# A two-layer decoder on one core: the causal mask added on two blocks instead of three, and one sum of each rotary job moved from VectorE to GpSimd

## The chip, the core and the metric

The kernel runs on one core of one Trainium2 chip. The metric is the device time of one execution in microseconds (us), the median of several. Engines are named as in the profile: PE is TensorE, PEld its weight loads, DVE is VectorE, ACT is ScalarE, POOL is GpSimd, SP is SyncE.

## What is computed

Two decoder layers on x (4 batches x 256 positions x 256). Each layer adds attention, a selective state space branch (fed by a context tensor and gated by x) and a feed-forward part. The change lies in attention 1, the attention of the second layer:

```python
qkv = einsum('bsh,oh->bso', x, w_qkv)          # 16 query heads, 4 key/value heads, 128 wide
q, k = layernorm(q, qn_g, qn_b), layernorm(k, kn_g, kn_b)      # per head
q = q * cos + rotate_half(q) * sin             # the same for k
scores = einsum('bhqd,bhkd->bhqk', q, k) / sqrt(D)
scores = where(causal, -inf, scores)           # 256 x 256, triu with k=1
attn = einsum('bhqk,bhkd->bhqd', softmax(scores), v)
x = x + einsum('bsd,od->bso', attn, w_o)
```

Beside it the kernel runs the state space branch of the same layer, a scan over 256 positions for each of 16 states of each batch:

```python
state = state * exp(d_t * A) + (d_t * u_t) * B_t;  y_t = sum_n(state * C_t)
```

## The kernel before, in words

The program is written by engine: each engine has one queue of instructions, carried out in order, with semaphores between engines. In attention 1 all five queues follow one list, `ATT1_PLAN`, that `att1_plan` (L1867) works out when the program is built. Every engine walks the list and issues its own part of each entry, so the list is the order on each queue.

**Units.** One unit is one head of one batch, 64 in all (`u` from 0 to 63). The scores of a unit are a [128, 384] piece of one PSUM bank: columns 0 to 127 are the first 128 queries against the first 128 keys, columns 128 to 383 the second 128 queries against all 256 keys. So two of the three 128 x 128 blocks lie on the diagonal. `s1` (L1711) first writes the mask there with a matmul of a bf16 identity and `mask1` (triangle, zeros, triangle; L1718, `start=True`), then adds the two fp32 products (L1719, L1720, `start=False`). `max1` (L1283) takes the two row maxima on DVE, `exp1` (L777) the exponentials on ACT, `norm1` (L1291) the reciprocal and two scalings on DVE (L1294, L1296, L1297), `pt1` transposes on PE, `pt_copy` copies on ACT (L791), `pv1` multiplies by V on PE, `at_copy` copies on ACT (L797), `o1` adds the output projection on PE (L1750).

**Slots.** The planner spreads these parts over slots. Slot u holds, in this order: the scores of unit u+1; the transposes of a rotary job and their copies, if one is due; norm of unit u-1; pv and copy of unit u-2; max and exp of unit u; o of unit u-3; a projection, if due; the accumulations of the state space steps of the slot before; ACT's decays; the transpose of unit u-1; then the rope, rot and sum parts that are due; last, the state space steps of this slot. So DVE starts each slot with norm of u-1 (which waits for exp of u-1) and max of u, and the start of L1294 number u-1 (from 0) is the start of DVE's slot u.

**Rotary jobs.** There are 20, five for each batch (one for the four key heads, four for the query heads, four heads each), in two tiles `job_a`, `job_b` of [128, 2, 512] fp32. `project` puts a job in PSUM (PE, L1671), ACT squares it (L757). Then DVE does `job` (two products with the tables, L1257, and L1261 twice), `job_sum` (sums of squares, L1269), and later `job_rope`: it adds `job_b` to `job_a` (L1274), waits for that sum and for the reciprocal standard deviations, and does eight multiply-adds (L1280). The standard deviations come from POOL, `job(j)` at L455: a scaling (L459) and a power (L460), started by the sums. PE transposes the job (L1708). A job projected in slot s has rot and sum in s+1, rope in s+3, transposes in s+5 (jobs 0 and 1, which run ahead of the first unit, have the rope in the slot right after the sum, and the second, at s-7, one slot later than the first). Jobs are due every third slot, for units of a batch that starts at slot 0: projections in 0, 3, 6, 9, a V projection in 12, and again one in 13.

**State space steps.** Steps 10 to 63 of the 64 quarter steps lie in attention 1. One step on DVE is a product (L997, into PSUM) and a scan (L1006). POOL then multiplies by C (`times_cq`, L403), and PE accumulates it (L1435). A `times_cq(q)` stands on POOL's queue where step q+1 stands in the list. SP loads the B and C rows, eight steps ahead.

**The planner's costs.** The planner gives DVE's parts a price in us (`rot` 2.6, `sum` 1.2, `rope` 3.2, `step` 2.0) and PE's load of each slot another. It hands out steps so that DVE's total, up to each slot, follows PE's (L1908 to L1947):

```python
spent += sum(price(p) for p in mine)
while ssm and spent + price(ssm[0]) / 2 < total * sum(load[:u + 1]) / sum(load):
    spent += price(ssm[0])
    now.append(ssm.pop(0))
```

For the kernel before, in the slots 0 to 15 of a batch: one step each in 0, 2, 3, 5, 6, 8, 9, 11, 12 and 15 and three in 13 (the same in the slots 16 to 47; from 48 one each in 48, 50, 51, 53, 55, 56, 57, two in 58, one each in 59, 60, 61 and three behind, two of them in 62 and one in 63).

Of the kernel before, what the change touches and what calls it, by code (L numbers as in the profile page):

```python
# [10 lines left out]
ALU = mybir.AluOpType  # L11
# [4 lines left out]
P = 128  # L16
# [73 lines left out]
def build(nc, io, out):  # L90
    ctx = ExitStack()
    with ctx:
        def sb(name, shape, dt=F32):
            return ctx.enter_context(nc.sbuf_tensor(name, shape, dt))

        def sem(name):
            return ctx.enter_context(nc.semaphore(name))
# [50 lines left out]
        identb = sb("identb", [P, P], BF16)  # L148
        mask0 = sb("mask0", [P, W0 + P], BF16)
        mask1 = sb("mask1", [P, 3 * P], BF16)  # L150
# [80 lines left out]
        job_a = lambda j: JA[j % 2]  # L231
        job_b = lambda j: V1[1] if j == 1 else JB
# [23 lines left out]
        ps = ctx.enter_context(nc.psum_tensor("ps", [P, 8, 512], F32))  # L256
# [22 lines left out]
        s = {n: sem(n) for n in names}  # L279
# [97 lines left out]
        def _(pool):  # L377
            gp = nc.gpsimd
# [76 lines left out]
            def job(j):  # L455

                pool.wait_ge(s["job_sum"], j + 1)
                st = jst[:, j % 2]
                ch.link(gp.tensor_scalar(st[:, 1, :], st[:, 0, :], 1.0 / D1, 1e-5, ALU.mult, ALU.add))  # L459
                gp.tensor_tensor(st[:, 2, :], st[:, 1, :], mhalf[:], ALU.pow).then_inc(s["job_rstd"], 1)  # L460

            for kind, a in ATT1_PLAN:
                if kind == "sum":
# [19 lines left out]
            z = slice(512, 1024)  # L483
# [405 lines left out]
        def _(dve):  # L889
            v = nc.vector  # L890
# [320 lines left out]
            step = iter(range(Q_IN_FFN))  # L1211
# [58 lines left out]

            def job_rope(b, i):
                j, x = JOB[b, i], 0 if i else 1
                dve.wait_ge(s["job_rot"], 3 * (j + 1))
                v.tensor_tensor(job_a(j), job_a(j), job_b(j), ALU.add).then_inc(s["job_add"], 1)  # L1274
                dve.wait_ge(s["job_add"], j + 1)
                dve.wait_ge(s["job_rstd"], j + 1)
                for t in range(2):
                    for h in range(REP1):
                        c = slice(D1 * h, D1 * h + D1)
                        v.scalar_tensor_tensor(job_a(j)[:, t, c], job_a(j)[:, t, c], jst[:, j % 2, 2, REP1 * t + h:REP1 * t + h + 1],  # L1280
                                               tabs[:, 3 * x + 2, t, :], ALU.mult, ALU.add).then_inc(s["job_rope"], 1)
# [48 lines left out]
            z = slice(0, 512)  # L1330
# [50 lines left out]
            with dve.Fori(0, E // WRING, 1) as i:  # L1381
                for k in range(WRING):
                    p = k % 2
# [12 lines left out]
        def _(pe):  # L1396
            mm, tr = nc.tensor.matmul, nc.tensor.transpose
# [170 lines left out]
            step = iter(range(6, LAYER_STEPS))  # L1568
# [53 lines left out]
            step = iter(range(Q_IN_FFN))  # L1622
# [88 lines left out]
            def s1(u):  # L1711
                b, h = u // H1, u % H1
                g, p = h // REP1, u % 2
                pe.wait_ge(s["job_tr_copied"], 2 * max(JOB[b, 0], JOB[b, 1 + g]) + 2)
                if u >= 2:
                    pe.wait_ge(s["s1_exp"], 2 * (u - 1))
                q, k = QT[(4 * b + g) % 2], KT[b % 2]
                mm(ps[:, 2 + p, 0:3 * P], identb[:], mask1[:], start=True, stop=True, skip_group_check=True)  # L1718
                mm(ps[:, 2 + p, 0:P], q[:, h % REP1, 0:P], k[:, g, 0:P], start=False, stop=True, skip_group_check=True)  # L1719
                mm(ps[:, 2 + p, P:3 * P], q[:, h % REP1, P:S], k[:, g, :], start=False, stop=True, skip_group_check=True).then_inc(s["s1_mm"], 1)  # L1720

# [145 lines left out]
def att1_plan():  # L1867
# [31 lines left out]
    for b in range(B):  # L1899
# [4 lines left out]
        if b + 1 < B:  # L1904
            rope_job(u + 6, b + 1, 0)
            rope_job(u + 9, b + 1, 1, 3, 4)
            v_job(u + 12, b + 1)
    cost = {"rot": 2.6, "sum": 1.2, "rope": 3.2, "step": 2.0}  # L1908
    ssm = [("da", (m, d)) for m in range(Q_IN_FFN, Q_IN_FFN + 3) for d in range(DT)]
    for m in range(Q_IN_FFN, QSTEPS):  # L1910
        if m + 3 < QSTEPS:
# [150 lines left out]
```

## Time and profile before

| what | us |
|---|---|
| median of 3 executions | 912.32 (912.07 to 913.70) |
| the profiled execution, its own time | 913.75 |
| its span, first to last instruction | 912.0 |
| DVE busy over the span | 703.3 (77%) |
| PE busy over the span | 767.7 (84%) |
| ACT busy | 445.6 (49%) |
| POOL busy | 340.6 (37%) |
| attention 1 (first L1671 to the last residual, L1319) | 334.9 to 674.3 |

Busy is the time with an instruction under way. A timeline row gives start, duration, engine, line, what it writes and reads, how many instructions are merged in it, and in brackets the idle time of that engine ahead of it with what ended it. Durations of neighbouring DVE instructions overlap a little, since the next begins while the last one drains; from start to start is the honest length.

### The profile page before, as it was taken

What the parts mean: (1) busy time and instruction counts of PE and PEld (TensorE: products, weight loads), DVE (VectorE), ACT (ScalarE), POOL (GpSimd) and SP (SyncE); (2) the same over time, 40 slices, a digit from 0 to 9 for tenths busy, and PEclk for the clock granted to TensorE, in tenths of its full rate; (3) what the DMA queues carried; (4) which work ended last, traced back from release to release, by engine and by line L of the source; (5) the groups of instructions that cost most, each with busy time, mean ns of one, the idle gap of its engine ahead of it and who ended that gap; (6) DMA issues with size and microseconds to landing.
All of it is one profiled execution on the core that took longest, in us unless ns stands there. A gap on an engine that the chain in (4) does not pass through costs nothing.

```text
span 912.0 us, 12288 instructions
## 1 busy us (share of the span) xinstructions
PE 767.7 (84%) x3984; PEld 563.1 (62%) x3984; DVE 703.3 (77%) x1229; ACT 445.6 (49%) x928; POOL 340.6 (37%) x242
## 2 busy tenths in 40 slices
PE   6771459877798996799999999999955799999997
PEld 2241346554433563477767776777743689999996
DVE  4869779889857976999999999999977544444443
ACT  1663368650336402666566556756642354444442
POOL 1001346552330422233333323432343286666663
PEclk9785579998799998999999999999987899999999
DMA  4313223345020212011111211111300243334431
GB/s 171 121 47 114 93 94 125 115 139 218 1 98 0 74 43 92 19 40 44 51 36 36 69 36 36 55 39 36 118 0 1 79 158 138 138 138 138 141 135 46
DMA packets 28884, 74.63 MB, mean 82 GB/s; under 512 B 3633, under 2 KB 6337, under 8 KB 28449
## 3 DMA queue, kind: packets, MB, share of 16 engines
q1 hardware_dynamic: 28384, 71.51, 23.2%
q10 hardware_dynamic: 448, 2.49, 0.8%
q8 instruction: 25, 0.41, 0.2%
q14 instruction: 27, 0.21, 0.1%
HBM read 72.55 MB, written 1.44 MB: 81 GB/s over the span
## 4 chain that ended last, share of the span: by engine, by line
PE 50%; DVE 26%; issue 11%; ACT 9%; POOL 3%; DMA 1%; POOLq 0%; DVEq 0%; SPq 0%; ACTq 0%
PE ps L1671 6%; PE ps L1785 6%; PE ps L1786 6%; PE ps L1787 6%; PE ps L1631 4%; DVE hS L976 3%; PE ps L1651 3%; PE ps L1750 3%; PE ps L1435 2%; PE ps L1738 2%; DVE arena L1280 2%; DVE hS L1006 2%; DVE ps L968 2%; PE ps L1408 1%; PE ps L1720 1%
## 5 line engine op out<-in xcount | busy, mean ns | idle before, releaser
L403 POOL TENSOR_TENSOR hS<-hS,BCb 128x512 f32<-128x512 f32 x64 | 81.6, 1278 | 131.9 <-issue 66.7
L1387 DVE SCALAR_TENSOR_TENSOR arena<-ps,arena 128x1024 f32<-128x1024 f32 x32 | 39.2, 1224 | 102.2 <-ACT arena L842 93.1
L426 POOL TENSOR_TENSOR hS<-hS,BCb 128x1024 f32<-128x1024 f32 x23 | 56.1, 2440 | 111.3 <-DVE ps L968 96.3
L1671 PE MATMUL ps<-WB,hT 128*128 128x512 f32 x192 | 88.0, 603 | 3.0 <-DVE arena L1261 2.0
L476 POOL TENSOR_TENSOR MHl<-arena,MHh 128x1024 fp32r<-128x1024 f32 x34 | 81.7, 2404 | 16.9 <-ACT MHh L845 16.9
L1416 PE MATMUL ps<-ident,hS 128*128 128x128 f32 x256 | 40.1, 311 | 54.7 <-POOL hS L426 31.2
L1785 PE MATMUL ps<-Wh,MHh 128*128 128x256 f32 x272 | 77.8, 286 | 6.0 <-POOL MHl L476 6.0
L1006 DVE TENSOR_TENSOR_SCAN hS<-dA,ps 128x512 f32<-128x512 f32 x64 | 78.1, 1220 | 2.2
L1786 PE MATMUL ps<-Wl,MHh 128*128 128x256 f32 x272 | 77.6, 285 | 0.0
L1787 PE MATMUL ps<-Wh,MHl 128*128 128x256 f32 x272 | 77.5, 285 | 0.0
L1416 PEld LDWEIGHTS ps<-ident,hS 128*128 128x128 f32 x256 | 32.6, 159 | 65.1 <-POOL hS L426 38.2
L473 POOL TENSOR_TENSOR Wl<-WB,Wh 128x512 fp32r<-128x512 f32 x34 | 47.3, 1392 | 64.2 <-ACT Wh L826 64.2
L1750 PE MATMUL ps<-WA,arena 128*128 128x256 f32 x256 | 65.7, 380 | 0.0
L1671 PEld LDWEIGHTS ps<-WB,hT 128*128 128x128 f32 x192 | 36.9, 194 | 40.6 <-issue 38.4
L976 DVE TENSOR_TENSOR_SCAN hS<-dA,ps 128x1024 f32<-128x1024 f32 x23 | 52.6, 2286 | 8.2 <-ACT dA L591 7.5
L1785 PEld LDWEIGHTS ps<-Wh,MHh 128*128 128x128 f32 x272 | 52.7, 194 | 8.3 <-POOL MHl L476 7.1
L605 ACT ACTIVATE dA<-DEL,negA 128x255 f32<-128x255 f32 x128 | 55.4, 504 | 0.0
L1785 PE MATMUL ps<-hTh,Wh 128*128 128x512 f32 x136 | 53.8, 396 | 0.0
L1786 PE MATMUL ps<-hTl,Wh 128*128 128x512 f32 x136 | 53.5, 394 | 0.0
L1786 PEld LDWEIGHTS ps<-Wl,MHh 128*128 128x128 f32 x272 | 52.8, 194 | 1.2
L1787 PE MATMUL ps<-hTh,Wl 128*128 128x512 f32 x136 | 53.1, 390 | 0.0
L1787 PEld LDWEIGHTS ps<-Wh,MHl 128*128 128x128 f32 x272 | 52.7, 194 | 0.0
(233 smaller groups left out, 1967.4 us busy)
## 6 DMA issues: line engine op xcount, KB each, us to landing
BCb<-bc_dram SPq DMA_DIRECT2D x32, 512.0 KB, 3.7
BCb<-bcq_dram SPq DMA_DIRECT2D x64, 256.0 KB, 3.1
arena<-gate_dram SPq DMA_DIRECT2D x32, 512.0 KB, 3.7
WB<-in_we SPq DMA_DIRECT2D x34, 256.0 KB, 2.7
WB<-in_wqkv SPq DMA_DIRECT2D x1, 3072.0 KB, 12.7
WA<-in_wo ACTq DMA_DIRECT2D x1, 2048.0 KB, 7.7
WA<-in_ffn SPq DMA_DIRECT2D x1, 1408.0 KB, 7.9
pkb<-in_pk SPq DMA_DIRECT2D x2, 698.0 KB, 4.7
```

The source lines that it names most:

```text
L403: gp.tensor_tensor(h, h, qbc(q)[:, 1:2, :].broadcast_to([P, DT, S]), ALU.mult).then_inc(s["c_ready"], 1)
L426: gp.tensor_tensor(h, h, BCb[g % SB_LOADS][:, 1:2, :].broadcast_to([P, DT, HALF]), ALU.mult).then_inc(s["c_ready"], 1)
L476: gp.tensor_tensor(MHl[:, p, :], MH[p], MHh[:, p, :].bitcast(F32), ALU.subtract).then_inc(s["m_lo"], 1)
L605: sc.activation(qring(dA, q)[:, d, 1:S], DEL[:, d, S * b + 1:S * b + S], ACT.Exp, scale=negA[:, d * DS + n:d * DS + n + 1]).then_inc(s["da ...
L976: v.tensor_tensor_scan(f(h), f(a), f(dbu(g)), 0.0, ALU.mult, ALU.add).then_inc(s["scan_done"], 1)
L1006: v.tensor_tensor_scan(f(qring(hS, q)), f(qring(dA, q)), ps[:, DBQ_BANK, :], 0.0, ALU.mult, ALU.add).then_inc(s["scan_done"], 1)
L1416: last = mm(ps[:, ACC_BANK + j // 2, 256 * (j % 2) + P * d:256 * (j % 2) + P * d + P], src[:, d, P * j:P * j + P], ident[:], start=(first ...
L1671: last = mm(ps[:, bank + t, :], hT[:, c, P * (2 * b + t):P * (2 * b + t) + P], WB[:, c, c0:c0 + 512], start=(c == 0), stop=(c == HC - 1))
L1750: last = mm(ps[:, 5, 256 * t:256 * t + 256], aT1[u % 2][:, P * t:P * t + P], WO1[:, h, :], start=(h == 0 and t == 0), stop=(h == H1 - 1), ...
L1785: mm(out, wh, xh, start=start, stop=False, **kw)
L1786: mm(out, wh, xl, start=False, stop=False, **kw)
L1787: return mm(out, wl, xh, start=False, stop=stop, **kw)
```

## The change

Three edits. The mask matmul writes and reads only blocks 0 and 2 of the three, through a strided view; its `start=True` stays. The sum `job_a + job_b` goes from DVE's `job_rope` to POOL's `job(j)`, behind the power, with the wait for the three products ahead of it; DVE keeps the wait for `job_add`. And the planner's price of `rope` goes from 3.2 to 2.1.

```diff
@@ POOL, job(j)
                 ch.link(gp.tensor_scalar(st[:, 1, :], st[:, 0, :], 1.0 / D1, 1e-5, ALU.mult, ALU.add))
                 gp.tensor_tensor(st[:, 2, :], st[:, 1, :], mhalf[:], ALU.pow).then_inc(s["job_rstd"], 1)
+                pool.wait_ge(s["job_rot"], 3 * (j + 1))
+                gp.tensor_tensor(job_a(j), job_a(j), job_b(j), ALU.add).then_inc(s["job_add"], 1)
@@ DVE, job_rope(b, i)
                 j, x = JOB[b, i], 0 if i else 1
-                dve.wait_ge(s["job_rot"], 3 * (j + 1))
-                v.tensor_tensor(job_a(j), job_a(j), job_b(j), ALU.add).then_inc(s["job_add"], 1)
                 dve.wait_ge(s["job_add"], j + 1)
                 dve.wait_ge(s["job_rstd"], j + 1)
@@ PE, s1(u)
-                mm(ps[:, 2 + p, 0:3 * P], identb[:], mask1[:], start=True, stop=True, skip_group_check=True)
+                diagonal = lambda z: z.rearrange("p (k n) -> p k n", k=3)[:, 0::2, :]
+                mm(diagonal(ps[:, 2 + p, 0:3 * P]), identb[:], diagonal(mask1[:]), start=True, stop=True, skip_group_check=True)
@@ att1_plan
-    cost = {"rot": 2.6, "sum": 1.2, "rope": 3.2, "step": 2.0}
+    cost = {"rot": 2.6, "sum": 1.2, "rope": 2.1, "step": 2.0}
```

The new price changes the list. By the planner's own sum, in slots 0 to 15 of a batch there are now one step each in 0 and 2, two each in 3, 6, 9 and 12, three in 13, and none in 5, 8, 11 and 15 (the same in the slots 16 to 47; from 48 one each in 48 and 50, two in 51, none in 52 to 54, two in 55, one each in 56 to 59, two in 60, one in 61 and two behind). Apart from what goes with a step (its decays, its accumulation), no other entry of the list moves. So of the three slots between one projection and the next, the slot with a rope holds two steps, the one with rot and sum none, as before, and the third none.

## Rows read from the trace of the kernel before

**Rows 1.** Stretches between starts of L1294: PE, weight loads, DVE, ACT, POOL, clock, DMA.

```profile
376.07:418.40 42.33, 40.86 (x213) 30.16 (x212) 41.70 (x97) 25.95 (x76) 13.45 (x12) 0.99 0.12 38
453.99:496.86 42.87, 41.84 (x223) 31.00 (x222) 42.24 (x98) 26.45 (x78) 13.47 (x12) 1.00 0.13 37
533.01:575.90 42.89, 41.85 (x223) 31.00 (x222) 42.26 (x99) 25.68 (x76) 13.46 (x12) 1.00 0.14 38
611.91:634.33 22.42, 21.89 (x124) 17.00 (x123) 22.04 (x55) 13.97 (x42) 7.69 (x7) 1.00 0.12 36
```

**Rows 2.** Timeline of DVE, slots 25 to 28: start us, us, what.

```profile
485.80 0.14 DVE L1294 RECIPROCAL rc<-sum 128x2 f32<-128x2 f32 x1
...
487.02 1.21 DVE L1274 TENSOR_TENSOR arena<-arena 128x1024 f32<-128x1024 f32 x1
488.26 2.19 DVE L1280 SCALAR_TENSOR_TENSOR arena<-arena,jst,tabs 128x128 f32<-128x128 f32 x8
490.37 0.69 DVE L997 TENSOR_TENSOR ps<-DU,BCb 128x512 f32<-128x512 f32 x1
...
492.23 0.14 DVE L1294 RECIPROCAL rc<-sum 128x2 f32<-128x2 f32 x1
...
496.86 0.15 DVE L1294 RECIPROCAL rc<-sum 128x2 f32<-128x2 f32 x1
...
497.71 0.42 DVE L1289 TENSOR_REDUCE nm<-ps 128x1 f32<-128x256 f32 x1
...
499.91 0.14 DVE L1294 RECIPROCAL rc<-sum 128x2 f32<-128x2 f32 x1
```

**Rows 3.** Timelines of ACT and POOL beside that, one row each.

```profile
498.88 0.20 ACT L784 ACTIVATION_READ_ACCUMULATOR arena<-ps,nm 128x1 f32 x1
...
497.31 1.78 POOL L460 TENSOR_TENSOR jst<-jst,mhalf 128x8 f32<-128x8 f32 x1
```

**Rows 4.** Groups by line and shape, POOL: count, busy us, mean ns, idle before.

```profile
L476 POOL TENSOR_TENSOR MHl<-arena,MHh 128x1024 fp32r<-128x1024 f32 x34 | 81.7, 2404 | 16.9 <-ACT MHh L845 16.9
...
L426 POOL TENSOR_TENSOR hS<-hS,BCb 128x1024 f32<-128x1024 f32 x23 | 56.1, 2440 | 111.3 <-DVE ps L968 96.3 <-issue 13.5 <-DVE hS L968 1.5
...
L445 POOL TENSOR_TENSOR WB<-WB,wmean 128x2560 f32<-128x2560 f32 x2 | 8.9, 4462 | 16.7 <-DVE wmean L1194 16.7
```

**Rows 5.** Line L1296: durations; then timeline rows of DVE and POOL where it was long.

```profile
L1296 DVE TENSOR_SCALAR arena<-arena,rc x64: 285/287/1358, 371.6 to 667.8; 128x128 f32<-128x128 f32 x64
...
667.61 0.14 DVE L1294 RECIPROCAL rc<-sum 128x2 f32<-128x2 f32 x1
667.78 1.36 DVE L1296 TENSOR_SCALAR arena<-arena,rc 128x128 f32<-128x128 f32 x1
...
666.57 2.48 POOL L403 TENSOR_TENSOR hS<-hS,BCb 128x512 f32<-128x512 f32 x2 [1.77 <-issue]
```

**Rows 6.** Timelines of POOL and DVE at 243 us, layer norm apply L1033.

```profile
243.27 3.66 POOL L440 TENSOR_TENSOR arena<-arena,dsc 128x256 f32<-128x256 f32 x5
...
241.99 1.05 DVE L1033 TENSOR_SCALAR H<-X,lnmv,lnrs 128x256 f32<-128x256 f32 x3
243.34 3.01 DVE L1033 TENSOR_SCALAR H<-X,lnmv,lnrs 128x256 f32<-128x256 f32 x4 [0.29 <-POOL lnrs L394]
```

**Rows 7.** Timeline of DVE, slot 62 into 63: two steps back to back.

```profile
660.65 0.69 DVE L997 TENSOR_TENSOR ps<-DU,BCb 128x512 f32<-128x512 f32 x1
...
664.58 0.14 DVE L1294 RECIPROCAL rc<-sum 128x2 f32<-128x2 f32 x1
```

**Rows 8.** Timeline of DVE: the rope of jobs 1 and 2.

```profile
353.95 2.19 DVE L1280 SCALAR_TENSOR_TENSOR arena<-arena,jst,tabs 128x128 f32<-128x128 f32 x8 [1.88 <-POOL jst L460]
...
367.47 2.19 DVE L1280 SCALAR_TENSOR_TENSOR arena<-arena,jst,tabs 128x128 f32<-128x128 f32 x8 [0.45 <-POOL jst L460]
```

**Rows 9.** The mask matmul: ns min, median, max, first and last start.

```profile
L1718 PE MATMUL ps<-mask,identb x64: 322/326/480, 360.6 to 659.7; 128*128 128x384 bf16 x64
```

**Rows 10.** Stretch of the prologue, with the granted clock (columns as Rows 1).

```profile
345.00:356.00 11.00, 7.09 (x16) 3.72 (x16) 8.83 (x21) 2.18 (x3) 2.92 (x3) 0.69 0.41 168
```

## The prediction

> **What bounds the kernel now.** I read the stretches of attention 1 first [rows 1]. Over three periods of three slots DVE is busy 42.24 of 42.87 us and PE 41.84. Both are full, so relief of one alone is worth little: the gain ends where PE's 41.84 / 3 = 13.95 us for a period begins. The timeline then shows what a slot of DVE is made of, from start to start [rows 2]. Norm and max take 1.22 (485.80 to 487.02), the sum of a rotary job 1.24, its eight multiply-adds 2.11, one step 1.86 (490.37 to 492.23), the slot with rot and sum 4.63 (492.23 to 496.86), the slot with a step alone 3.05. A period is 499.91 - 485.80 = 14.11 us. Two steps in a row take 660.65 to 664.58, 3.93 us [rows 7].
>
> The third view is the other engines beside that [rows 3]. POOL's power L460 ends at 497.31 + 1.78 = 499.09, which is 2.2 us after DVE began the slot behind the sums of squares. ACT ends exp at 499.08, also 2.2 us after it. Both are hidden today, because DVE has 3.05 us of work in that slot, and a norm and a max in the next, before anyone needs them.
>
> **The change, part by part.**
>
> *DVE loses the sum.* 20 times 1.24 us, 24.8 in all, if nothing replaced it.
>
> *POOL gains it, and it is a link of a chain.* Two SBUF operands of 128x1024 fp32, written back in place. The nearest rows are L476 at 2404 ns, which has the same operands but for the output's type, and L426 at 2440 ns; L445, an add whose second operand repeats, needs 4462 ns for 2560, which is 1.78 us for 1024 [rows 4]. I take 2.37 us, since two full operands are like the first two (and L426's mean holds a long one), and keep 1.78 and 2.44 as ends. By the Trainium skill, page "GPSIMD Engine Reference", section "Elementwise — side-by-side cycle accounting", an add of 2048 fp32 takes 4497 ns; half of it, an estimate of 2.25 us, would make 20 sums 2.4 us cheaper together. The measured rows decide. The rope waits for the sum, the sum follows the power on POOL's queue: it ends at 2.2 + 2.37 = 4.57 us after the start of the slot behind the sums of squares. POOL has no backlog: it is busy 13.47 of 42.87 us [rows 1], and of the C products queued behind a sum, one started by a step of slot 2 is late by the rest of the sum, where PE needs it only at the end of the next slot. No DMA moves, neither SP's nor ACT's queue is passed, and SP's loads run eight steps ahead.
>
> *The steps leave the third slot.* With `rope` at 2.1 that slot keeps norm and max, 1.22 us. Now the next norm waits for exp, 2.2 us after the slot's start. Then comes the norm's L1296, 0.17 us later, and POOL is in the middle of its sum.
>
> *DVE and POOL in the same memory.* L1296 takes 287 ns, but 1358 once: it began at 667.78, with a POOL product of 1.27 us that began at about the same time and ended at 666.57 + 2.48 = 669.05; L1296 ended at 669.14 [rows 5]. At 243 us the same form, L1033, takes 0.35 us each where it is undisturbed and 3.01 / 4 = 0.75 beside five POOL products [rows 6]. So such a scaling waits until the streaming POOL instruction is over. I take it that L1296 waits for the end of the sum, at 4.57; what is left of norm and max, 1.22 - 0.17 - 0.2, brings the rope to 5.4 us after the slot's start. Ends: no block, and the rope starts at 4.57 + 0.1; a block behind a longer sum, 5.5.
>
> *A period after.* 5.4 to the rope, 2.11 for it, 3.93 for two steps, 4.63 for rot and sum: 16.07 us against 14.11. PE has 13.95 of work in it and waits.
>
> *Sum over attention 1.* Three such periods in each of batches 0 to 2: 48.2 against 42.33, 42.87 and 42.89 [rows 1] is +16.5. The seven slots from slot 11 of a batch to slot 2 of the next hold 5.4 + 2.11 + 3.93 (slots 11 and 12), 7.2 (norm, max, three steps), 4.63, 5.4 + 2.11 + 1.86 (slots 15 and 16) and 4.63, 37.3 in all. Before they took what lies between the stretches: 35.59 (418.40 to 453.99), 36.15 and 36.01 [rows 1]; together +4.1. From slot 50 to 55, 5.4 + 2.11 + 3.93 + 4.63 + 5.4 + 2.11 = 23.6 against 22.42: +1.2. At the end two steps stand where three stood: between -2.07 and 0, I take -1.0. Jobs 0 to 2 run ahead of the units with nothing between sums and rope: DVE already waited 1.88 us for POOL at job 1 and 0.45 at job 2 [rows 8], and PE, ACT and DVE wait for each other in turn there, so each sum adds its 2.37 in full: +7.1. Together +27.9.
>
> *The mask.* 128 of 384 bf16 columns fewer, 64 times. The matmul is 326 ns [rows 9]; a third of that is 0.11 us, at most 7 us in all and at least 0. I take 0: the cover is DVE's longer period, in which PE waits 2 us. If DVE were not the bound, PE would keep some of it.
>
> Against the profiled execution's 913.75 the sum gives 941.6; the median of the runs is 1.4 lower, and against it the sum gives 940.
>
> **The rivals.**
>
> *No block.* The scaling runs beside the sum; the rope starts at 4.67. Each of some 17 exposed chains in the units is 0.7 us shorter: 940 - 12 = 928. For it: L1296's median is 287 ns although POOL is busy a third of the time [rows 1, 5]. Against it: rows 5 and 6. By the Trainium skill, page "SBUF — State Buffer", section "Who interferes with whom", the two engines share a port pair as an exclusive lock and the second blocks fully, which would leave this rival nothing; the trace agrees where it shows the case.
>
> *A faster sum.* At L445's rate all 20 chains are 0.59 shorter: 940 - 12 = 928.
>
> *The clock.* PE idles longer. In the prologue the granted clock was 0.69 over 11 us in which PE was busy 7.1 [rows 10]. If such stretches spread (the low level is half the high one), each costs PE a few us that DVE's slack no longer hides. At 2 us for three of them in the prologue and 2 more: 950.
>
> *The other side: the chain stays hidden.* One place decides, DVE's wait for `job_add` ahead of the rope. If POOL's chain ended within what DVE has to do before the rope (3.5 us after the slot's start: 2.2, then norm and max), the period would be DVE's 14.11 - 1.24 plus about 1.0 for exp, 13.9, or PE's 13.95 less a mask saving. 9 periods times 0.2 are 1.8, the mask and the last slots may give 2 to 3 more: 908. It needs the sum in under 1.3 us; the cheapest row says 1.78.
>
> *It all cancels.* Planner slack and mask meet the waits to within 0.2%, about what a measurement of this kernel can tell from no change. Nothing in the rows speaks for it.
>
> **How the numbers follow.** Forecast 0.60, no block 0.11, faster sum 0.12, clock 0.10, hidden 0.05, cancels 0.02. The predicted time is the likeliest, 940; its own range is 934 to 945. The range reaches to both rivals at 928 and a part of the clock's: 926 to 948. Slower by more than 0.2% is 0.93, within it 0.02, faster 0.05.
>
> **What would show it.** Right: DVE idle ahead of L1280 with POOL's new line as the releaser, or L1296 long (1 to 2.4 us) in about one slot of three; from L1294 to L1294 three slots on 16.1 us in the regular stretch; a new POOL group x20 at 2.3 to 2.5 us; PE busy in attention 1 down from 98% to under 90%; nothing changed after attention 1. Wrong: L1296 at 0.3 us throughout; a POOL sum under 2 us; L1280 with no idle ahead of it in slots 3, 6, 9 and 12; or periods of 14 us.

## The result: 3.6% slower, and the profile after

| | median, us | from, to | runs |
|---|---|---|---|
| before | 913.01 | 912.07 to 916.04 | 4 |
| after | 945.29 | 944.53 to 949.96 | 4 |

The ratio is 1.0358, with a 95% interval of 1.0316 to 1.0401. The change costs 32 us where 27.9 were forecast; 945.29 lies inside the range of 926 to 948 and just above the forecast's own range of 934 to 945. The profiled execution took 944.78 us with a span of 942.7.

The first view of the kernel after is the page's head with the busy times: engine, busy us, share of the span, instructions.

```profile
span 942.7 us, 12288 instructions
...
PE 771.2 (82%) x3984; PEld 559.6 (59%) x3984; DVE 710.8 (75%) x1209; ACT 447.6 (47%) x928; POOL 386.7 (41%) x262
```

DVE lost 20 sums of 1.24 us, about 25 us of work, and yet is busy longer, 710.8 against 703.3 us. That is the riddle which the next views solve: an instruction that is blocked counts as busy. The two scalings of norm, L1296 and L1297, are busy 29 us longer in all, 71.2 us against 42.1.

The second view is the table of stretches, columns as in Rows 1; first attention 1 as a whole before, then the same after.

```profile
339.63:673.60 333.97, 308.90 (x1602) 227.93 (x1600) 312.88 (x692) 193.43 (x560) 107.97 (x94) 0.98 0.16 48
```

```profile
338.23:704.03 365.80, 314.36 (x1602) 224.18 (x1600) 320.21 (x673) 195.61 (x560) 154.06 (x114) 0.98 0.14 44
...
380.50:429.57 49.07, 42.06 (x218) 30.07 (x217) 46.24 (x97) 26.40 (x76) 21.77 (x16) 0.99 0.12 38
466.68:515.73 49.05, 43.07 (x224) 30.45 (x223) 46.22 (x98) 26.02 (x76) 21.78 (x16) 1.00 0.11 38
554.36:603.42 49.06, 43.54 (x230) 31.17 (x229) 46.23 (x98) 26.05 (x76) 21.78 (x16) 1.00 0.12 38
640.56:665.06 24.50, 21.23 (x117) 15.64 (x116) 23.14 (x53) 13.71 (x41) 12.39 (x9) 1.00 0.14 33
```

The whole growth lies in attention 1: 365.80 - 333.97 = 31.8 us. From the last residual to the end of the span it is 238.6 us after and 238.4 before. The four lower rows answer to [rows 1]: three regular periods now take 49.06 us where they took 42.3 to 42.9. PE is busy 43.07 of 49.05 us there, 88%, against 98%, at full clock: it waits. DVE is still 94% busy.

The third view is the timeline of DVE in slots 23 to 26 after, which answers to [rows 2]: start, duration, engine, line, what.

```profile
495.10 0.14 DVE L1294 RECIPROCAL rc<-sum 128x2 f32<-128x2 f32 x1
...
499.72 0.16 DVE L1294 RECIPROCAL rc<-sum 128x2 f32<-128x2 f32 x1
...
501.98 0.17 DVE L1294 RECIPROCAL rc<-sum 128x2 f32<-128x2 f32 x1 [0.98 <-ACT arena L786]
502.18 2.19 DVE L1296 TENSOR_SCALAR arena<-arena,rc 128x128 f32<-128x128 f32 x1
504.30 0.34 DVE L1297 TENSOR_SCALAR arena<-arena,rc 128x256 f32<-128x256 f32 x1
...
505.09 2.17 DVE L1280 SCALAR_TENSOR_TENSOR arena<-arena,jst,tabs 128x128 f32<-128x128 f32 x8
507.19 0.69 DVE L999 TENSOR_TENSOR ps<-DU,BCb 128x512 f32<-128x512 f32 x1
...
511.11 0.14 DVE L1294 RECIPROCAL rc<-sum 128x2 f32<-128x2 f32 x1
```

Beside it the timeline of POOL in the same stretch, which answers to [rows 3].

```profile
500.17 1.80 POOL L460 TENSOR_TENSOR jst<-jst,mhalf 128x8 f32<-128x8 f32 x1
501.94 2.35 POOL L462 TENSOR_TENSOR arena<-arena 128x1024 f32<-128x1024 f32 x1
508.01 1.27 POOL L403 TENSOR_TENSOR hS<-hS,BCb 128x512 f32<-128x512 f32 x1 [3.72 <-DVE ps L999]
```

A period is 511.11 - 495.10 = 16.01 us. The third slot begins at 499.72 and holds only norm and max, 2.26 us with a wait of 0.98 for exp. The next norm begins at 501.98, just when POOL starts the sum (501.94), and its first scaling, L1296, does not end before the sum does: 502.18 + 2.19 = 504.37 against 501.94 + 2.35 = 504.29. The rope follows at 505.09, 5.37 us after the third slot began; 5.4 was forecast. There is no idle time ahead of the rope: the wait for POOL hides inside a busy scaling of DVE.

The fourth view is the count of single lines after: ns min, median, max, first and last start.

```profile
L462 POOL TENSOR_TENSOR arena<-arena x20: 2337/2348/2353, 343.7 to 659.8; 128x1024 f32<-128x1024 f32 x20
...
L1296 DVE TENSOR_SCALAR arena<-arena,rc x64: 285/288/2204, 376.1 to 697.7; 128x128 f32<-128x128 f32 x64
...
L1297 DVE TENSOR_SCALAR arena<-arena,rc x64: 340/348/1378, 376.3 to 698.9; 128x256 f32<-128x256 f32 x64
...
L1719 PE MATMUL ps<-mask,identb x64: 269/273/372, 362.7 to 690.7; 128*128 128x256 bf16 x64
```

The sum costs 2.348 us on POOL, the mask matmul lost 53 ns of its 326 [rows 9]. The medians of both scalings are undisturbed; only their maxima tell of the block. In this trace 17 scalings begin while the sum is under way, one for each job whose rope lies in the units. Every one of them ends within 0.1 us behind the sum.

### The profile page after: what moved, and what is told of

Read it like the earlier page. It is cut to its first block, busy times and chain, and to the rows that moved or that the text cites. A ratio compares the mean times of both kernels' runs of the same rounds, so it can differ in the third digit from the quotient of the medians.

```text
span 942.7 us, 12288 instructions
## 1 busy us (share of the span) xinstructions
PE 771.2 (82%) x3984; PEld 559.6 (59%) x3984; DVE 710.8 (75%) x1209; ACT 447.6 (47%) x928; POOL 386.7 (41%) x262
## 4 chain that ended last, share of the span: by engine, by line
PE 38%; DVE 36%; issue 13%; ACT 8%; POOL 3%; DMA 0%; DVEq 0%; POOLq 0%; SPq 0%; ACTq 0%
PE ps L1786 6%; PE ps L1787 6%; PE ps L1788 6%; DVE hS L1008 5%; DVE arena L1280 4%; PE ps L1631 4%; DVE ps L999 3%; DVE hS L978 3%; PE ps L1651 3%; DVE arena L1263 2%; DVE jst L1271 2%; DVE arena L1259 2%; PE ps L1671 2%; DVE nm L1289 2%; DVE ps L970 2%
## 5 line engine op out<-in xcount | busy, mean ns | idle before, releaser
L403 POOL TENSOR_TENSOR hS<-hS,BCb 128x512 f32<-128x512 f32 x64 | 81.6, 1278 | 116.6 <-DVE ps L999 77.5
L1671 PE MATMUL ps<-WB,hT 128*128 128x512 f32 x192 | 90.0, 615 | 3.1 <-DVE arena L1263 2.1
```

Source lines behind the costliest of these rows:

```text
L403: gp.tensor_tensor(h, h, qbc(q)[:, 1:2, :].broadcast_to([P, DT, S]), ALU.mult).then_inc(s["c_ready"], 1)
L1671: last = mm(ps[:, bank + t, :], hT[:, c, P * (2 * b + t):P * (2 * b + t) + P], WB[:, c, c0:c0 + 512], start=(c == 0), stop=(c == HC - 1))
```

## The experiments

All the regular stretches below are the nine slots 18 to 27 (three periods) of each kernel, from start to start of the norm's reciprocal; before they take 42.87 us, after 49.05.

### The mask alone

The kernel before with this one edit:

```diff
-                mm(ps[:, 2 + p, 0:3 * P], identb[:], mask1[:], start=True, stop=True, skip_group_check=True)
+                diagonal = lambda z: z.rearrange("p (k n) -> p k n", k=3)[:, 0::2, :]
+                mm(diagonal(ps[:, 2 + p, 0:3 * P]), identb[:], diagonal(mask1[:]), start=True, stop=True, skip_group_check=True)
```

> The kernel before with the mask edit alone (two blocks of 128 columns instead of 384 columns). Theory A (the mask is worth nothing, because what follows it on TensorE, the pv of unit u-2, waits for a copy on ScalarE in most slots, and DVE's period of 14.1 us bounds the rest): 912 to 913, ratio 1.000 +- 0.002, the mask matmul at 273 ns instead of 326, the period of three slots still 14.1 us. Rival B (TensorE is the bound and every one of the 64 matmuls gives back its 53 ns or more): 905 to 909.

Measured: 913.44 us against 914.23 of the kernel before in the same session, ratio 0.9999 (0.9978 to 1.0020). The regular stretch takes 42.88 us, as before. A third of the columns is worth nothing that can be measured while DVE sets the period: 64 times 53 ns are 3.4 us of PE's work, and it goes into PE's waits.

### The planner's price alone

The kernel before with this one edit; the sum stays on DVE.

```diff
-    cost = {"rot": 2.6, "sum": 1.2, "rope": 3.2, "step": 2.0}
+    cost = {"rot": 2.6, "sum": 1.2, "rope": 2.1, "step": 2.0}
```

> The kernel before with the planner's price alone (rope 2.1 instead of 3.2); the sum stays on DVE, the mask is whole. Theory A (the loss has two parts that each cost by themselves, and an empty third slot makes DVE wait for exp): a regular period of 2.26 (empty slot) + 1.22 + 1.24 + 2.11 + 3.93 + 4.63 = 15.4 us instead of 14.1, about +15 us in all, 924 to 930, L1294 with some 13 idle times ahead of it that end with ScalarE, L1296 at 0.29 us throughout. Rival B (the planner's price is harmless without the GpSimd sum): 912 to 915.

Measured: 935.69 us, ratio 1.0225 (1.0181 to 1.0269); the expected time was too low. The regular stretch came as expected, 47.45 us, a period of 15.37 (one chain: wait for exp, norm, max, then the sum of 1.24 and the rope, two steps). L1294 waited 16 times for ScalarE, and L1296 was at 287 ns but for the one long instance that the kernel before has too. The miss sits where one batch follows the other: slots 27 to 34 took 41.59 us against 36.15 before. Two views of this kernel show what is different there. First the stretches there, columns as in Rows 1:

```profile
526.00:530.00 4.00, 0.97 (x7) 0.57 (x4) 2.44 (x7) 4.00 (x9) 1.23 (x1) 0.90 0.57 130
530.00:536.40 6.40, 6.24 (x24) 5.59 (x25) 4.48 (x9) 1.30 (x6) 1.98 (x2) 0.53 0.02 5
536.40:545.00 8.60, 8.33 (x40) 5.79 (x39) 5.25 (x16) 4.81 (x16) 0.00 (x0) 1.00 0.00 0
```

Then DVE's timeline at the end of it:

```profile
539.65 0.17 DVE L1294 RECIPROCAL rc<-sum 128x2 f32<-128x2 f32 x1 [5.13 <-ACT arena L784]
```

PE is busy only 0.97 of 4.00 us up to 530.00; it waits 3.19 us of them for a copy on ACT (L791). Behind that its granted clock is 0.53, about the low of the two levels (1.2 against 2.4 GHz), while it is busy 6.24 of 6.40 us, and DVE, which lives on its results by way of ACT, waits 5.13 us for exp. The forecast had named this danger in the clock's rival, but for the prologue.

### The sum on POOL alone

The kernel before with the sum moved and the price left at 3.2, so that the list of entries stays as it was.

```diff
@@ POOL, job(j)
+                pool.wait_ge(s["job_rot"], 3 * (j + 1))
+                gp.tensor_tensor(job_a(j), job_a(j), job_b(j), ALU.add).then_inc(s["job_add"], 1)
@@ DVE, job_rope(b, i)
-                dve.wait_ge(s["job_rot"], 3 * (j + 1))
-                v.tensor_tensor(job_a(j), job_a(j), job_b(j), ALU.add).then_inc(s["job_add"], 1)
```

> The kernel before with the sum on GpSimd alone (price 3.2, mask whole). Theory A: the step that stays in the third slot covers exp, but the product of that step queues behind the sum on GpSimd, so L1296 waits for the end of the sum and L1297 for the product: 6.4 us from the third slot's start to the rope, a period of 6.4 + 2.11 + 1.86 + 4.63 = 15.0 us, +5.8 in the prologue, 927 to 933 in all. Rival B (with the steps left where they were, three slots hide the sum and DVE is relieved by 1.24 us a job): 905 to 912 with periods of 14.0. Rival C (the sum alone is the whole loss of the change): 940 to 946.

Measured: 931.32 us, ratio 1.0193 (1.0151 to 1.0236), regular stretch 44.94 us, 14.98 for a period, as expected. With a step in the third slot DVE comes to the norm later, but both scalings are blocked; timelines of DVE and POOL in slot 25 of this kernel:

```profile
496.39 0.14 DVE L1294 RECIPROCAL rc<-sum 128x2 f32<-128x2 f32 x1
...
496.57 1.43 DVE L1296 TENSOR_SCALAR arena<-arena,rc 128x128 f32<-128x128 f32 x1
...
497.92 1.37 DVE L1297 TENSOR_SCALAR arena<-arena,rc 128x256 f32<-128x256 f32 x1
```

```profile
495.56 2.35 POOL L462 TENSOR_TENSOR arena<-arena 128x1024 f32<-128x1024 f32 x1
...
497.87 1.26 POOL L403 TENSOR_TENSOR hS<-hS,BCb 128x512 f32<-128x512 f32 x1
```

L1296 ends with the sum (498.00 and 497.91). The product L403 of a step had queued behind the sum, starts at once and ends at 499.13; L1297 ends at 499.29. So the sum costs DVE 1.1 us directly and 1.0 more by the product that it holds up; the 1.24 us saved do not pay for the two. Both are held like this in all 17 slots of this kind.

### The change with norm's reciprocals in PSUM

This is the test of the block. In the change, the reciprocals go into two columns of a PSUM bank, and the two scalings become products with a PSUM operand. Waits are added because the bank is shared with the steps. So the edit alters two things at once: where the reciprocal lies, and the kind of instruction.

```diff
-                v.reciprocal(rc1[:, p, :], sum1[:, p, :]).then_inc(s["s1_rc"], 1)
+                dve.wait_ge(s["scan_done"], LAYER_STEPS + steps[0])
+                rc = ps[:, DBQ_BANK, 0:2]
+                v.reciprocal(rc, sum1[:, p, :]).then_inc(s["s1_rc"], 1)
...
-                v.tensor_scalar(P1[p][:, 0:P], P1[p][:, 0:P], rc1[:, p, 0:1], None, ALU.mult).then_inc(s["s1_norm"], 1)
+                v.tensor_tensor(P1[p][:, 0:P], P1[p][:, 0:P], rc[:, 0:1].broadcast_to([P, P]), ALU.mult).then_inc(s["s1_norm"], 1)
```

(and the same for the second scaling; a step waits for the last norm).

> The changed kernel with the two scalings of norm (L1296, L1297) in another form: the reciprocals lie in PSUM and a tensor_tensor multiplies by them, so that DVE has one SBUF input and runs in its plain mode; everything else as in the change. The second scaling takes about 0.07 us more. Theory A (L1296 is long because both engines want the same SBUF port): the scalings are at 0.3 and 0.4 us everywhere, DVE idles ahead of the rope for the rest of the sum instead, the regular period is 4.65 + 2.11 + 3.93 + 4.63 = 15.3 to 15.5 us instead of 16.0, the time 930 to 937. Rival B (a streaming GpSimd instruction stops every DVE instruction on SBUF data, or the long rows are an artefact of the profile): scalings still long, or short with the time unchanged, 944 to 950.

Measured: 944.10 us (937.56 to 947.26), ratio 1.0318 (1.0257 to 1.0379): as a time the expectation of 930 to 937 missed, and 944 is where the rival had put it. The rows it named came out. Counts of the two scalings, then DVE's timeline in the slot of the rope and POOL's beside it, all of this kernel:

```profile
L1300 DVE TENSOR_TENSOR arena<-arena,ps x64: 286/288/291, 381.3 to 697.8; 128x128 f32<-128x128 f32 x64
...
L1301 DVE TENSOR_TENSOR arena<-arena,ps x64: 411/414/417, 381.5 to 698.1; 128x256 f32<-128x256 f32 x64
```

```profile
503.52 0.17 DVE L1298 RECIPROCAL ps<-sum 128x2 f32<-128x2 f32 x1 [0.98 <-ACT arena L786]
503.73 0.29 DVE L1300 TENSOR_TENSOR arena<-arena,ps 128x128 f32<-128x128 f32 x1
...
505.65 2.19 DVE L1280 SCALAR_TENSOR_TENSOR arena<-arena,jst,tabs 128x128 f32<-128x128 f32 x8 [0.76 <-POOL arena L462]
```

```profile
503.26 2.35 POOL L462 TENSOR_TENSOR arena<-arena 128x1024 f32<-128x1024 f32 x1
```

Not one of 128 scalings is blocked, although 34 of them begin while the sum is under way, and the wait has moved to where it belongs: DVE idles 0.76 us for L462 ahead of the rope. The regular stretch is 47.30 us, and slots 2 to 55 together are 8 us shorter than in the change. Why the time did not show more of it: the new norm has a price of its own, which the control below measures; the first rotary work up to slot 2 took 2.0 us longer than after, the last part 2.3; and the granted clock was lower. The four executions had a mean granted clock of 0.918, 0.913, 0.911 and 0.926 and took 943.88, 944.32, 947.26 and 937.56 us. Three of the change's four had 0.925 to 0.927 and took 944.53 to 945.81. At the same clock the PSUM norm is thus 7 to 8 us faster, though only one execution says so. The profiled one had 0.96 in slots 2 to 11 and again from slot 55 on, where the change had 0.99 and 1.00.

The same rows show a difference of kind. For 128 columns more the plain scaling takes 60 ns longer (288 to 348), the new form 126 (288 to 414), so the plain form works at about twice the rate. Whether the second SBUF operand or this faster kind of work is what gets it blocked, the test can't tell, since both went together.

### The control: the same norm in the kernel before

The edit of the last experiment, made in the kernel before.

> Control for the two kernels whose norm goes by PSUM: the kernel before with that alone. The second scaling takes 0.41 instead of 0.35 us and the reciprocal waits for the last scan; 0.07 to 0.11 us for each of 64 units on a DVE that is the bound: period 14.4 us, slots 2 to 11 in 43.2 us instead of 42.3 to 42.9, 915 to 920. If DVE were not the bound: 912 to 914.

Measured: 922.90 us (921.93 to 923.82), ratio 1.0100 (1.0083 to 1.0117): it costs more than expected. The slots take 6.68, 4.73 and 3.31 us where they took 6.43, 4.62 and 3.05. The regular stretch is 44.91 us; a slot with a rope and a step is 0.25 longer, though the scalings take only 0.07 us more together. The slot with a step alone is 0.26 longer as well, the slot with rot and sum and no step only 0.11. That fits the norm's wait for the last scan, which the plain form need not make; it was not tried by itself.

With this control the block can be priced. By the medians the change costs 944.1 - 922.9 = 21.2 us on the PSUM norm and 32.3 on the plain one, a block of 11 us, give or take some 7 by the intervals of the ratios, and three of the four executions behind the 944.1 ran at a lower clock. The traces are less disturbed. In slots 2 to 55 the change adds 26.3 us on the plain norm and 8.5 on the PSUM norm, which makes 18. That takes the new norm to cost as much in the change as in the kernel before, although there its price may vanish in waits; if it cost nothing there, the block would be the plain difference of 8. So it is worth 8 to 18 us. The rival without a block had said 12 us less than the forecast.

### The change with next to no sum

```diff
-                gp.tensor_tensor(job_a(j), job_a(j), job_b(j), ALU.add).then_inc(s["job_add"], 1)
+                gp.tensor_tensor(job_a(j)[:, :, 0:4], job_a(j)[:, :, 0:4], job_b(j)[:, :, 0:4], ALU.add).then_inc(s["job_add"], 1)
```

This kernel leaves out most of the sum: only 8 of the 1024 elements of a partition are added.

> The changed kernel with GpSimd's sum cut from 1024 elements a partition to 8, so most of the rotary sum is left out; list, price, mask and every wait as in the change. Theory A (what the price alone costs is DVE's time: two steps and the sum in a row; without the sum the empty slot just reaches TensorE's 14 us): prologue back to 36 to 38 us from the first L1259 (rot) to the norm of slot 2, slots 2 to 11 in 43 to 44.5 us instead of 49.1, L1296 at 0.29 us, 910 to 916. Rival B (the empty slot, its wait for exp, is the loss, whatever the sum does): 924 or more.

Measured: 918.58 us (916.95 to 925.30), ratio 1.0056 (1.0035 to 1.0077), a little above the expectation. This bounds the whole idea: even if POOL's sum cost almost nothing, this list of entries would be slower than before. The regular stretch is 43.97 us, since DVE still waits for exp in the thinned slot, and slots 27 to 34 took 41.88 us at a mean clock of 0.92, the disturbance of the price experiment again. The profiled execution is the longest of the seven, 925.30 us, so the median holds less of this than the trace. The scaling first, then the stretches, all of this kernel:

```profile
L1296 DVE TENSOR_SCALAR arena<-arena,rc x64: 285/286/1362, 373.2 to 677.0; 128x128 f32<-128x128 f32 x64
```

```profile
458.14:502.11 43.97, 42.07 (x226) 30.89 (x224) 40.80 (x98) 25.49 (x75) 15.27 (x16) 1.00 0.15 43
502.11:543.99 41.88, 37.52 (x179) 27.22 (x177) 30.75 (x73) 22.36 (x64) 11.89 (x12) 0.92 0.13 39
```

(slots 18 to 27 and 27 to 34.) With every wait and every entry of the list as in the change, L1296 is long only once, at the same place as in the kernel before [rows 5]: it is the length of the sum that blocks, not the new order. Against the change this kernel is 27 us faster, so 27 of the 32 us hang on what the sum does on POOL.

### The change with the sum ahead of the power

The sum needs only the three products, the power needs DVE's sums of squares. So in the change the two swap places on POOL's queue:

```diff
             def job(j):
+                pool.wait_ge(s["job_rot"], 3 * (j + 1))
+                gp.tensor_tensor(job_a(j), job_a(j), job_b(j), ALU.add).then_inc(s["job_add"], 1)
...
                 gp.tensor_tensor(st[:, 2, :], st[:, 1, :], mhalf[:], ALU.pow).then_inc(s["job_rstd"], 1)
-                pool.wait_ge(s["job_rot"], 3 * (j + 1))
-                gp.tensor_tensor(job_a(j), job_a(j), job_b(j), ALU.add).then_inc(s["job_add"], 1)
```

> The changed kernel with GpSimd's sum ahead of the scaling and the power, so that it starts when the three products are done, beside DVE's sums of squares, and not 3.3 us later. Theory A (chain and port together): the rope can start 3.4 us after the third slot's start instead of 5.4; L1296 of the third slot waits 1.1 us for the rest of the sum, and exp behind it by as much, so the period is 3.4 + 1.2 + 2.11 + 3.93 + 4.63 = 15.3 us instead of 16.0; prologue 1.1 us shorter a job; slots 2 to 11 in 47 us instead of 49.1; 929 to 936. Rival B (the length of the chain from the sums of squares does not matter, only that GpSimd streams): no change, 943 to 948.

Measured: 933.94 us (933.47 to 935.28), ratio 1.0223 (1.0201 to 1.0246), as expected; 11 us less than the change. The period is 15.09 us. DVE's timeline of this kernel from the sums of squares to the norm behind them, POOL's beside it:

```profile
507.13 1.21 DVE L1271 TENSOR_REDUCE jst<-arena 128x8 f32<-128x1024 f32 x1
...
508.45 1.29 DVE L1296 TENSOR_SCALAR arena<-arena,rc 128x128 f32<-128x128 f32 x1
```

```profile
507.29 2.37 POOL L458 TENSOR_TENSOR arena<-arena 128x1024 f32<-128x1024 f32 x1 [3.43 <-DVE arena L1263]
```

The first 1.1 us of the sum run beside the sums of squares L1271, which is not slowed at 1.21 us, and only the rest falls on a scaling, at the start of the third slot instead of the slot behind it: 1.29 us instead of 2.19, 17 times. The chain is no longer what the rope waits for.

### Two versions meant to win

Both put back the price 3.2, keep the mask edit, keep the sums of jobs 0 to 2 (the prologue) on DVE and put the other 17 on POOL, ahead of the power:

```diff
+                if j >= 3:
+                    pool.wait_ge(s["job_rot"], 3 * (j + 1))
+                    gp.tensor_tensor(job_a(j), job_a(j), job_b(j), ALU.add).then_inc(s["job_add"], 1)
```

The first has the PSUM norm in every unit.

> A version that might beat both: mask on two blocks, price 3.2 (steps as before), the sum on GpSimd ahead of the power for jobs 3 to 19, on DVE for jobs 0 to 2, where nothing hides it, and norm's scalings by reciprocals in PSUM, so that they don't share the port. Theory A: nothing is exposed any more, DVE has 14.1 - 1.24 + 0.3 = 13.2 us of work in a period, TensorE's 13.9 is the bound: slots 2 to 11 in 41.9 to 42.3 us, prologue as before, 907 to 912. Rival B (a streaming GpSimd instruction costs DVE time in other ways as well): 914 or more.

Measured: 914.71 us (911.89 to 915.66), ratio 1.0002 (0.9990 to 1.0014), not the 907 to 912 that was expected. The regular stretch came as expected, 41.93 us; from slot 55 to the last residual it lost 1.2 (40.51 against 39.27).

The second has the PSUM norm only in the two norms behind a job's sums, where POOL's sum runs, and the plain one elsewhere.

```diff
+                if near[0]:
+                    near[0] -= 1
...
+                    if JOB[a] >= 3:
+                        near[0] = 2
```

> The combination of before (mask on two blocks, price 3.2, the sum of jobs 3 to 19 on GpSimd ahead of the power) with the PSUM form of norm only in the two norms that follow the sums of squares of such a job, and the plain form in all others. Theory A (TensorE bounds the regular periods at 41.9 us for three, the slower norm cost 1.2 us in the tail and some tenths at the ends of batches): slots 2 to 11 as in the combination, 41.9 to 42.3, the tail from slot 55 back at 39.3, in all 333.97 - 3 = 331 from the first rot to the last residual, 910 to 913, ratio 0.996 to 0.999. Rival B (relief of DVE is not worth anything measurable once TensorE is the bound): ratio 1.000 +- 0.001.

Measured: **910.55 us** (908.60 to 913.26, 12 runs) against 914.42, ratio 0.9959 (0.9943 to 0.9975). This is inside the expectation of 910 to 913, and it beats both kernels. Its stretches, slots 18 to 27 and 27 to 34, columns as in Rows 1:

```profile
453.49:495.44 41.95, 41.01 (x218) 30.18 (x217) 39.85 (x95) 26.17 (x78) 21.34 (x16) 1.00 0.14 38
495.44:531.82 36.38, 35.13 (x186) 25.74 (x185) 32.98 (x74) 21.77 (x63) 18.04 (x14) 1.00 0.17 52
```

PE is busy 41.01 of 41.95 us and DVE 39.85: the bound has changed engines, and a period of 13.98 is what the forecast had called the end of any gain (13.95 us). DVE is busy 2.4 us less than before [rows 1], and the stretch is 0.9 us shorter. With PE as the bound, the mask edit may be worth something here that it was not worth alone: nine slots at 53 ns are 0.5 us of this 0.9. No run has this kernel with the whole mask, so how the gain divides between mask and sum is not shown.

### The same without the PSUM norm

> Control for the kernel with the PSUM form in two norms of three: the same (mask on two blocks, price 3.2, the sum of jobs 3 to 19 on GpSimd ahead of the power), but every norm in the plain form with its two scalings from SBUF. Theory A (the port is what eats DVE's relief): the scaling that follows the sums of squares waits 1.1 us for the rest of GpSimd's sum, another may wait for the product of a step, DVE has 14.1 - 1.24 + 1.1 to 2.3 = 14.0 to 15.2 us of work in a period, slots 2 to 11 in 42.5 to 45.5 us instead of 41.9, 914 to 924. Rival B (the form of the scalings does not matter, the place of the sum does): slots 2 to 11 in 41.9 us, 909 to 912.

Measured: 915.69 us (914.48 to 916.21), ratio 1.0018 (1.0007 to 1.0029), regular stretch 42.83. DVE's and POOL's timeline in slot 27 of this kernel:

```profile
497.88 1.29 DVE L1300 TENSOR_SCALAR arena<-arena,rc 128x128 f32<-128x128 f32 x1
```

```profile
496.72 2.35 POOL L459 TENSOR_TENSOR arena<-arena 128x1024 f32<-128x1024 f32 x1 [3.73 <-DVE arena L1264]
```

The block takes 1.0 us of DVE's time at each of the 17 jobs. Where PE is nearly the bound, 0.3 us of that reach each period, and the gain is gone: the ratios 1.0018 and 0.9959 differ by 0.6%, some 5 us, and that decides the sign.

## Why the prediction was right

**The period.** Forecast 16.07 us, measured 16.01, by the very chain that was written down: third slot thinned to norm and max, next norm behind exp, L1296 blocked to the end of POOL's sum, rope 5.37 us after the third slot's start (5.4). The two-step slot and the rot slot kept their lengths. The forecast named the signs of being wrong too (L1296 at 0.3 us throughout, periods of 14); the PSUM norm brought the first about, and the period fell to 15.4. One sign on that list did come true and says nothing against the mechanism: L1280 has no idle ahead of it in slots 3, 6, 9 and 12. The forecast's own working hides the wait inside L1296, so that sign was ill chosen.

**The sum on POOL.** Taken at 2.37 us from the rows with two full operands [rows 4], measured 2.348 (2.337 to 2.353). The choice between the ends 1.78 and 2.44 was right: the add with the repeated operand was no guide. The rival that built on it falls.

**The block.** The step that rested on one long scaling and a slowed neighbour [rows 5, rows 6] held: 2.2 us at L1296 in two of the three periods of a regular stretch, 0.8 and then 1.4 at L1297 in the first. In the four kernels with the plain norm and the sum on POOL (the change, the sum alone, the sum ahead of the power, the last control), each of the 68 scalings that begin beside a sum ends within 0.1 us behind it; of the 68 in the PSUM form, in two kernels, none is held. By the Trainium skill, page "SBUF — State Buffer", section "Who interferes with whom", DVE in a 2-port mode, or with two SBUF inputs where the GpSimd instruction reads SBUF, and a GpSimd instruction take a shared port pair in turn, and the second one waits for the whole of the first. By that rule, the traces agree at all three points where it says something: L1296 ends with the sum, the scalings with a PSUM operand are never held (288 and 414 ns), and the reduce L1271 runs beside the sum at its usual 1.21 us.

**Terms that were mis-sized.** The total is a little luckier than its parts: the prologue was put 1.3 us too high, the regular stretches 2.6 too low. Measured as differences of the same starts in the two traces:

| stretch | before | after | difference | forecast |
|---|---|---|---|---|
| first rot to slot 2 | 36.44 | 42.27 | +5.8 | +7.1 |
| slots 2 to 11, 18 to 27, 34 to 43 | 128.10 | 147.17 | +19.1 | +16.5 |
| slots 11 to 18, 27 to 34, 43 to 50 | 107.75 | 112.88 | +5.1 | +4.1 |
| slots 50 to 55 | 22.42 | 24.50 | +2.1 | +1.2 |
| slot 55 to the last residual | 39.27 | 38.97 | -0.3 | -1.0 |
| all | 333.97 | 365.80 | +31.8 | +27.9 |

The regular stretches hold one step that the forecast missed. It said of the products queued behind the sum only that one would be late for PE, which "needs it only at the end of the next slot". In slot 3 of a batch (19, 35, 51) the product of slot 2's step stands behind the sum, starts when it ends, and blocks the second scaling as the sum blocked the first. DVE's and POOL's timeline after, slot 19:

```profile
466.68 0.15 DVE L1294 RECIPROCAL rc<-sum 128x2 f32<-128x2 f32 x1
...
470.50 0.83 DVE L1296 TENSOR_SCALAR arena<-arena,rc 128x128 f32<-128x128 f32 x1
471.25 1.37 DVE L1297 TENSOR_SCALAR arena<-arena,rc 128x256 f32<-128x256 f32 x1
...
473.07 2.17 DVE L1280 SCALAR_TENSOR_TENSOR arena<-arena,jst,tabs 128x128 f32<-128x128 f32 x8
```

```profile
468.89 2.35 POOL L462 TENSOR_TENSOR arena<-arena 128x1024 f32<-128x1024 f32 x1
471.20 1.27 POOL L403 TENSOR_TENSOR hS<-hS,BCb 128x512 f32<-128x512 f32 x1
```

The rope starts 473.07 - 466.68 = 6.39 us after the third slot's start, 1.0 us more than in the other periods, though that slot kept its step. The forecast had taken all three periods of a stretch as 16.07 (48.2 together); the first is 17.0, the stretch 49.06. This is 2.6 us over the three stretches, and with slot 51, where it comes back, it is also what slots 50 to 55 took beyond their term. Of the stretches between batches two took 37.1, where 37.3 was forecast; the third (27 to 34) took 38.6, with 5.59 us instead of 4.63 in slot 30, a place that the forecast had not looked at by itself.

**The prologue.** Three sums were to add 2.37 each. Ropes 0 to 2 after, DVE's timeline:

```profile
346.12 2.19 DVE L1280 SCALAR_TENSOR_TENSOR arena<-arena,jst,tabs 128x128 f32<-128x128 f32 x8 [3.74 <-POOL arena L462]
...
356.13 2.19 DVE L1280 SCALAR_TENSOR_TENSOR arena<-arena,jst,tabs 128x128 f32<-128x128 f32 x8 [4.36 <-POOL arena L462]
...
371.91 2.19 DVE L1280 SCALAR_TENSOR_TENSOR arena<-arena,jst,tabs 128x128 f32<-128x128 f32 x8 [3.84 <-POOL arena L462]
```

The mechanism is right: here the rope does idle for L462, 11.9 us in three waits. From the sums of squares to the rope it is now 5.55 to 5.58 us each time, and was 3.32, 4.22 and 3.32: two jobs pay 2.2 us. The middle one pays 1.4, because POOL's scaling had taken 1.10 us there before, and 0.20 in its usual place. It had begun behind DVE's own sum (350.85 to 352.07) and ended with it, at 352.12: the block in the other direction, which goes once that sum has left DVE. The three together are 5.85 us, the whole of the measured 5.8.

**The mask.** Costed at nothing, and nothing by itself. The cover named, DVE's longer period, is real: PE waits 6 us in a stretch of 49.

**The rivals.** No block: excluded by the rows of L1296, and worth 8 to 18 us where it had been priced at 12. Hidden chain: the sum would have had to end within 3.5 us and ended at 4.57; with almost no sum the kernel was still 0.6% slower, so this rival was dearer than its 908 us even on its own ground. The clock: in the stretch that answers to [rows 10] it fell further, to 0.58, as the stretches after show,

```profile
345.00:356.00 11.00, 7.36 (x16) 3.83 (x16) 5.65 (x12) 1.41 (x3) 5.15 (x4) 0.58 0.33 140
```

but the prologue took no more than its sums explain. At the batch border the change keeps 1.00; three of the variants (the price alone, next to no sum, sum ahead of the power) took 4 to 7 us more there than at their own other two borders, and their mean clock over that stretch was 0.92, 0.92 and 0.96.

**Who costs what.** The mask 0, the moved sum alone +17, the price alone +21, all three +32, less than their sum. Some 5 of the price's 21 are the disturbance at the batch border, which the change did not have. In the regular periods the two add almost in full, 0.9 and 1.3 us against 1.9 together. The two edits that belong together in the planner's eyes each do harm alone. The price is an honest estimate of the rope's cost to DVE, and the planner is blind to what it moves: with it the third slot loses its step, which had hidden exp and POOL's chain.

**What stays open.** With the PSUM norm PE was granted less clock in three executions of four, for which the traces give no cause. And what in the timing makes PE fall to the low clock at the batch border in three variants and not in the change was not settled.

## What to carry to other kernels

Moving work from a full engine to an idle one paid here only when the idle engine's chain ended before its taker arrived and when DVE ran nothing meanwhile that gets blocked. Ask what DVE runs in the microseconds in which the moved instruction streams. The scaling with both operands in SBUF was held each time; the product with one operand in PSUM and the reductions were not. So change the form of what runs there, or place the move beside one of these. When a planner's price is corrected, read the new list and not only the new cost, because the filler it moves may have been the cover of another engine's latency. A line's maximum duration, not its median or its idle time, shows such a block; engine busy time goes up with it.

## What the runs showed that was not expected

- A short POOL instruction is held up by DVE as well. In the fastest version, POOL's scaling of 8 elements took 0.64 us beside DVE's product of two SBUF operands (L1000, 496.74 to 497.43) where it takes 0.20 alone, and so at all 17 jobs of the units:

```profile
496.84 0.64 POOL L462 TENSOR_SCALAR jst<-jst 128x8 f32<-128x8 f32 x1
```

- POOL's power of 8 elements takes 1.65 us here and 1.80 in the change, where it starts at 500.17, within a scaling of DVE (500.12 to 500.47). In the change all 17 that begin within a scaling take 1.79 to 1.80 us, the three of the prologue that do not take 1.64 or 1.65. The 0.15 us look like a wait for DVE, though the rest of that scaling was 0.30; that was not tested by itself.
- A multiply-add of the rope, with two operands in SBUF, can be held too: in the fastest version the first of the eight takes up to 0.53 us, where the median is 0.34, when a product of POOL (L403) is still under way.
- The norm with a PSUM operand costs DVE 0.07 us more in its scalings and yet 0.25 us more per slot with a step, 8.8 us over the kernel. Used in 34 of 64 units it paid; used in all it did not.
- At the batch border of the price experiment PE was busy 0.97 of 4.00 us, then had a granted clock of 0.53 over 6.40 us in which it was busy 6.24, then 1.00. At the full level the same work would have taken about 3.3 us, an estimate from these shares, so the low clock cost some 3 us at one place.
